# Graph network on one Trainium2 core: a head of three tiles in place of four in the second half of the adjacency stage

## What is computed

```python
h = relu(layernorm(x));  x = x + gcn2(relu(gcn1(h)))      # two GCN layers, the same edges
h = relu(layernorm(x))
w = silu(edge_attr @ We1 + be1) @ We2 + be2
m = w * (h[src] @ Wlin)
x = x + h + silu(segment_sum(m, dst) @ Wn1 + bn1) @ Wn2 + bn2
```

## The kernel before, in words

| blocks | windows | 2 tiles | 3 tiles | 4 tiles | 5 or more |
|---|---|---|---|---|---|
| 0 to 24 | 200 | 0 | 3 | 67 | 130 |
| 25 to 48 | 192 | 1 | 130 | 60 | 1 (the last window: 6) |

## Time and profile before

### The profile page before, as it was taken

One profiled execution on the slowest core, in us unless ns is written; L12 is line 12 of the kernel. 1 busy time (PEld: TensorE's weight loads), 2 busy tenths in 40 slices (PEclk: granted clock), 3 DMA queues, 4 the chain that ended last, 5 costly groups with the idle time before them and its releaser, 6 DMA issues.

```text
span 3517.3 us, 70075 instructions
## 1 busy us (share of the span) xinstructions
PE 2970.2 (84%) x19882; PEld 2165.5 (62%) x19883; DVE 2086.3 (59%) x4759; ACT 959.0 (27%) x2055; POOL 1494.5 (42%) x1601
## 2 busy tenths in 40 slices
PE   6979999999999969978877777778778778777777
PEld 4742456777777769955555555555555555555555
DVE  7999999999999844444443344433444334443333
ACT  5110234455666511122222222122122222122221
POOL 0000000000000000057777777777777777777774
PEclk8989999999999989978788888887788888888888
DMA  2000011222222269833333333333333333333332
GB/s 62 0 0 1 38 56 74 93 93 107 111 111 110 108 267 346 323 79 80 76 80 79 79 77 79 80 79 78 78 80 79 79 79 79 77 79 80 77 76 67
DMA packets 278864, 324.81 MB, mean 92 GB/s; under 512 B 231024, under 2 KB 238345, under 8 KB 266143
## 3 DMA queue, kind: packets, MB, share of 16 engines
q1 hardware_dynamic: 227518, 217.13, 18.6%
q0 software_dynamic: 51168, 106.07, 11.8%
HBM read 238.00 MB, written 85.09 MB: 92 GB/s over the span
## 4 chain that ended last, share of the span: by engine, by line
POOL 41%; PE 35%; issue 17%; DVE 5%; DVEq 1%; POOLq 1%; ACT 0%; DMA 0%; SPq 0%; ACTq 0%
POOL shared L497 41%; PE pb L1294 9%; PE pa L1294 9%; PE pc L1288 6%; PE pd L1288 5%; PE pd L1252 3%; PE pf L1254 1%; PE pb L1379 1%; DVE shared L952 1%; DVE loop L952 1%; PE pb L1506 0%; PE pa L1372 0%; DVEq L952 0%; PE pb L1262 0%; DVE loop L957 0%
## 5 line engine op out<-in xcount | busy, mean ns | idle before, releaser
L497 POOL DMA_INDIRECT shared<-lin_table,idx x1568 | 1479.6, 944 | 479.0 <-issue 477.5
L1115 DVE TENSOR_TENSOR shared<-pb,shared 128x512 f32<-128x512 f32 x392 | 252.4, 686 | 1171.8 <-DMA shared<-lin_table,idx 1171.8
L526 POOL DMA_DIRECT2D lin_table<-c x12 | 9.2, 770 | 1498.9 <-issue 1308.6
L1453 PE MATMUL pb<-we_sb,shared 128*128 128x128 f32 x3136 | 619.8, 359 | 0.0
L1453 PEld LDWEIGHTS pb<-we_sb,shared 128*128 128x128 f32 x3136 | 526.3, 254 | 119.6 <-issue 119.1
L729 ACT ACTIVATE shared<-pa,be_col 128x512 f32<-128x512 f32 x392 | 247.9, 683 | 1101.7 <-PE pa L1442 1101.7
L1449 PE MATMUL pb<-be_parts,ones 3*128 3x512 bf16 x392 | 177.9, 454 | 404.9 <-DVE shared L1115 404.5
L952 DVE TENSOR_SCALAR shared<-col_h,shared 128x784 bf16<-128x784 f16 x1092 | 402.7, 416 | 5.0 <-issue 4.5
L1449 PEld LDWEIGHTS pb<-be_parts,ones 3*128 3x128 bf16 x392 | 36.5, 93 | 467.8 <-issue 451.0
L1442 PE MATMUL pa<-shared,we_sb 64*128 64x512 f32 x784 | 306.8, 870 | 0.7 <-ACT shared L724 0.7
L1294 PE MATMUL pb<-shared,c 128*128 128x392 bf16 x1568 | 304.0, 329 | 1.6 <-DVE shared L952 0.9
(11 more groups left out here) (233 smaller groups left out, 3813.5 us busy)
## 6 DMA issues: line engine op xcount, KB each, us to landing
adjacency<-shared SPq DMA_DIRECT2D x49, 1568.0 KB, 5.6
shared<-adjacency SPq DMA_DIRECT2D x49, 1568.0 KB, 8.4
shared<-in_edge_attr_dram SPq DMA_DIRECT2D x195, 256.0 KB, 3.0
shared<-lin_table,idx POOLq DMA_INDIRECT x1568
lin_table<-c POOLq DMA_DIRECT2D x12, 256.0 KB, 6.9
out_dram<-xr SPq DMA_DIRECT2D x12, 256.0 KB
shared<-in_dst_dram SPq DMA_DIRECT2D x1, 512.0 KB
shared<-in_src_dram SPq DMA_DIRECT2D x1, 512.0 KB
```

The lines of the kernel that those rows point to most:

```text
L497: pool.indirect_dma_start(out=dest(s, j), out_offset=None, in_=table, in_offset=bass.IndirectOffsetOnAxis(ap=idx[:, s, j:j + 1], axis=0)). ...
L1115: dve.tensor_tensor(msgs[s % 2][:, h, :, :], pb[:, h, :].rearrange("p (i f) -> p i f", f=F), rows[:, h, :, :], ALU.mult).then_inc(msg_read ...
L1453: last = pe.matmul(pb[:, h, i * F:(i + 1) * F], act_t[:, h, i * P:(i + 1) * P], we2_sb[:, :], start=False, stop=(i == 3))
```

## The change

From block 25 on (SHORT) the head has three tiles (SHORT_HEAD). `head_columns(1)` and PE's second head part do one tile there. What a window has more than three is done as one tile by itself (`single`), and what is more than four in the loop of four. `sources` of the head is as wide as before (four tiles). The block loop is written twice, with 12 turns each: blocks 1 to 24 with the old form, blocks 25 to 48 with the new. The tables are written with two instructions each, one for each range of blocks.

```diff
+SHORT = 25
+SHORT_HEAD = 3
...
+        def late_heads(b, short):
+
+            return b * WB + SHORT * WB if short else b * (WB * T)
...
             for n in range(2):
                 dve.wait_ge(test_used, (n + 1) * UCOLS)
                 of = span_ps[n].rearrange("a (b w) -> a b w", w=WB)
-                to = windows[:, 0:NB, n, :]
-                if n == 0:
-                    dve.tensor_scalar(to, of, float(UNITS - HEAD), None, ALU.min).then_inc(windows_ready, 1)
-                else:
-                    dve.tensor_scalar(to, of, -float(HEAD), 0.0, ALU.add, ALU.max).then_inc(windows_ready, 1)
+                for blocks, head in ((slice(0, SHORT), HEAD), (slice(SHORT, NB), SHORT_HEAD)):
+                    to = windows[:, blocks, n, :]
+                    if n == 0:
+                        dve.tensor_scalar(to, of[:, blocks, :], float(UNITS - head), None, ALU.min).then_inc(windows_ready, 1)
+                    else:
+                        dve.tensor_scalar(to, of[:, blocks, :], -float(head), 0.0, ALU.add, ALU.max).then_inc(windows_ready, 1)
...
-            def build_block(b, i, k, first=False):
+            def build_block(b, i, k, first=False, short=False):
+                head = SHORT_HEAD if short else HEAD
...
                     def head_columns(j):
-                        for t in range(T):
+                        for t in range(head - T if j else T):
                             columns(head_col[w % 2][j][:, t, :], i, first_tile, j * T + t, w).then_inc(head_hot[j], 1)
...
                         for o in range(2):
+                            if short:
+                                dve.wait_ge(tile_hot[o][0], units[o])
                             dve.wait_ge(tile_hot[o][T - 1], units[o])
...
+                    def single(e, u, ahead):
+                        dve.reg_add(units[e], units[e], 1)
+                        dve.wait_ge(tile_used[e][0], units[e])
+                        columns(loop_col[e][:, 0, :], i, u, ahead, w)
+                        dve.wait_ge(tile_used[e][1], units[e])
+                        sources(loop_lo[e], iota_t, u, ahead, T).then_inc(tile_hot[e][0], 1)
+                        dve.sem_inc(tile_hot[e][1], 1)
+
                     with dve.If_lt(spans[w], spans[WB + w]):
-                        odd_pair(dve, lead, start, spans[w], spans[WB + w])
-                        with dve.If_ne(lead, 0):
-                            loop_pair(w % 2, first_tile, HEAD)
+                        if short:
+                            single(w % 2, first_tile, head)
+                            dve.reg_add(start, spans[w], 1)
+                        else:
+                            odd_pair(dve, lead, start, spans[w], spans[WB + w])
+                            with dve.If_ne(lead, 0):
+                                loop_pair(w % 2, first_tile, head)
                         with dve.If_lt(start, spans[WB + w]):
...
-            with nc.Fori(0, NB // 2, engines=bass.OrderedEngineSet([dve.engine]), hint_back_edge=True) as it:
-                build_block(it * 2 + 1, 1, it)
-                build_block(it * 2 + 2, 0, it + 1)
+            for turns, short in (((0, SHORT // 2), False), ((SHORT // 2, NB // 2), True)):
+                with nc.Fori(*turns, engines=bass.OrderedEngineSet([dve.engine]), hint_back_edge=True) as it:
+                    build_block(it * 2 + 1, 1, it, short=short)
+                    build_block(it * 2 + 2, 0, it + 1, short=short)
...
+                    def single(e):
+                        pe.reg_add(units[e], units[e], 1)
+                        pe.wait_ge(tile_hot[e][0], units[e])
+                        tile_counts(ps, loop_lo[e][:, :, 0], loop_col[e][:, 0, :]).then_inc(tile_used[e][0], 1)
+                        pe.wait_ge(tile_hot[e][1], units[e])
+                        pe.sem_inc(tile_used[e][1], 1)
+
                     with pe.If_lt(ranges[w], ranges[WB + w]):
-                        odd_pair(pe, lead, start, ranges[w], ranges[WB + w])
-                        with pe.If_ne(lead, 0):
-                            loop_pair(w % 2)
+                        if short:
+                            single(w % 2)
+                            pe.reg_add(start, ranges[w], 1)
+                        else:
+                            odd_pair(pe, lead, start, ranges[w], ranges[WB + w])
+                            with pe.If_ne(lead, 0):
+                                loop_pair(w % 2)
```

More of the change, by code:

```diff
@@ L54 @@
 assert N_NODES <= PAD_DST
+assert SHORT % 2 == 1 and SHORT_HEAD == T + 1
 def gnn_kernel(nc, x, src, dst, edge_attr, W1, b1, W2, b2, We1, be1, We2, be2, Wlin, Wn1, bn1, Wn2, bn2, out):
@@ L941, in _ @@
             lead, start = dve.alloc_register("lead_dve"), dve.alloc_register("start_dve")
-            dve.wait_ge(windows_ready, 2)
+            dve.wait_ge(windows_ready, 4)
             for t in range(HEAD):
@@ L975, in build_block @@
                     if w == 0 and not first:
-                        dve.wait_ge(head_hot[1], b * (WB * T))
+                        dve.wait_ge(head_hot[1], late_heads(b, short))
                         dve.sem_inc(passed, 1)
                         for o in range(2):
+                            if short:
+                                dve.wait_ge(tile_hot[o][0], units[o])
                             dve.wait_ge(tile_hot[o][T - 1], units[o])
@@ L1236, in _ @@
             pe.wait_ge(w_loaded, 16 * (N_W - 3))
-            pe.wait_ge(windows_ready, 2)
+            pe.wait_ge(windows_ready, 4)
             pe.sem_inc(hist_used, RING - 1)
@@ L1295, in tile_counts, with head_counts, build_block @@
                 return last
-            def head_counts(ps, n, w, j):
-                for t in range(T):
-                    pe.wait_ge(head_hot[j], n * T + (t + 1))
+            def head_counts(ps, b, w, j, short):
+                tiles = SHORT_HEAD - T if short and j else T
+                for t in range(tiles):
+                    if j:
+                        pe.wait_ge(head_hot[j], late_heads(b, short) + (w * tiles + t + 1))
+                    else:
+                        pe.wait_ge(head_hot[j], b * (WB * T) + (w * T + t + 1))
                     last = tile_counts(ps, head_lo[w % 2][:, :, j * T + t], head_col[w % 2][j][:, t, :],
-                                       first=(j == 0 and t == 0), end=(j == 1 and t == T - 1))
+                                       first=(j == 0 and t == 0), end=(j == 1 and t == tiles - 1))
                 return last.then_inc(head_used[j], 1)
-            def build_block(b, i, first=False):
+            def build_block(b, i, first=False, short=False):
                 window_spans(pe, ranges, b)
@@ L1309, in build_block @@
                     pe.sem_inc(passed, 1)
-                    head_counts(ps, b * WB + w, w, 0)
+                    head_counts(ps, b, w, 0, short)
                     def loop_pair(e):
@@ L1324, in build_block @@
                                 loop_pair(w % 2)
-                    head_counts(ps, b * WB + w, w, 1)
+                    head_counts(ps, b, w, 1, short)
                     if w > 0 and not first:
@@ L1333, in _ @@
             pe.wait_ge(split_ready[0], 2)
-            with nc.Fori(0, NB // 2, engines=bass.OrderedEngineSet([pe.engine]), hint_back_edge=True) as it:
-                build_block(it * 2 + 1, 1)
-                build_block(it * 2 + 2, 0)
+            for turns, short in (((0, SHORT // 2), False), ((SHORT // 2, NB // 2), True)):
+                with nc.Fori(*turns, engines=bass.OrderedEngineSet([pe.engine]), hint_back_edge=True) as it:
+                    build_block(it * 2 + 1, 1, short=short)
+                    build_block(it * 2 + 2, 0, short=short)
             pe.wait_ge(win_out, NW + 2)
```

11 lines of the change are left out of this document (6 added, 5 removed).

## The result

The changed kernel takes **3494.3 us** (median of 4 runs, 3492.9 to 3496.1) against 3518.1 for the kernel before beside it (3516.6 to 3520.3): ratio 0.9936, 95% interval 0.9924 to 0.9948. It is faster, by 23.8 us; the forecast was 31, and its range of 3475 to 3500 holds the time. The profiled execution took 3496.07, its span 3494.4.

The account below looks back on a forecast made before the run. PE's gapless matmuls were taken to bound blocks 25 to 48. The 42.9 us saved, less 10.8 for block steps, 0.5 for DVE, 0.5 for the second loop and 0.2 for tables, gave 31 us: 3487.6 us, range 3475 to 3500.

Parts of the forecast that it names:

- Tiles left out: Blocks 25 to 48: 641 tiles in place of 770, so PE loses 42.9 us on the path that sets the end.
- The step from block to block: PE's sequencer between blocks no longer covered by queued matmuls: loss of 10.8 us, bounds 0 and 14.4.
- The second loop: Step from the first block loop into the second: 0.5 us lost, bounds 0 and 2.2, a gain excluded.
- The branch and the single tile: Windows of four entering the branch body on both engines: 0 inside a block, upper bound 13 us.
- DVE's excess: Blocks where DVE's work exceeds PE's: 0.5 us in the sum, bounds 0 and 2.6.
- rival 2: DVE and PE, near equal, hold each other up: 25 us lost, 3501 us, or 3494 if half the blocks; chance 0.20.
- The tables: Two instructions of 0.55 us become four of about half the length: 0.2 us lost, bounds 0 to 0.5.
- The stages behind: Stages after the adjacency stage start earlier and keep their length; a change of length would prove the forecast wrong.
- Rival 1: All of the tiles' gain arrives, block steps being hidden: 3475.8 us, up to 3481 with small terms; chance 0.20.
- Rival 3: Each of 60 windows' jumps into fresh code stalls: at 1.5 us a window 47 us slower, 3566 us; chance 0.05.

Follow-up runs that it names:

- fourth_counts_pad: Changed kernel with lighter fourth tile, PE's load of 8 numbers instead of 16, and 64 never-run instructions between DVE's two loops: 3481.9 us, ratio 0.9888.
- ahead3: Changed kernel with PE's load of the next block's 16 bounds moved from the block's start to behind window 3: 3496.8 us, ratio 0.9940.
- two_loops: Kernel before with DVE's and PE's block loop each written twice, old form of block in both, no tile left out: ratio 1.0047.
- fourth: Changed kernel with the fourth tile's sources taken from the head's own tile and its columns put into the head's free buffer: ratio 0.9983.
- fourth_counts: Changed kernel with the lighter fourth tile and PE's load of 8 numbers instead of 16, no padding: 3500.8 us, ratio 0.9952.
- fourth_pad: Changed kernel with the lighter fourth tile and 64 never-run instructions between DVE's two loops: 3486.3 us, ratio 0.9912.

## Why the prediction was right, and where it was off

- **Tiles left out, 42.9 us: right to the tile.** 2035 `columns`, and fourth_counts_pad comes to within 10 us of the stretch that PE's work alone would take. The path was right too: PE's stream sets the stretch, and what was lost are waits in it.
- **The step from block to block: right in kind, mis-sized.** "I take 0.45 x 24 = 10.8 us; bounds 0 and 0.6 x 24 = 14.4". The gaps are 16.7 us, of which 1.8 are block 25's entry and 14.9 the other 23 steps. The place and the cause are the predicted ones: halving the load took 10 us from these gaps. At the even blocks the measured 0.47 is what was taken. The odd ones have 0.83, and there PE's sequencer has 0.55 us more to do, the turn of its loop. The rows that the sum was read from stand at the start of block 26, an even one, and so leave it out; the 0.60 of the earlier trace rows, put down to the branch, stands at block 15, behind such a turn. ahead3 adds that PE has so little handed over in windows of three tiles that the load bares it at another place as well.
- **The second loop: the term that failed most.** "The step from one loop into the other has no row [...] Taken: 0.5, nearer the bottom as the next code simply follows", with a top of 2.2. It cost 3.3 us of DVE's time at once, block 25 had 4.0 us of excess, eight times what was taken and above the top, and two_loops puts it on the second copy alone (3.8). "A gain there is excluded" held. The turns of the second loop had no term at all; in the changed kernel they stayed at 0.48 to 0.87 us, six of eleven as in the first loop (0.47 to 0.54), while in three other layouts (two_loops, fourth, fourth_counts) they took 2.0 to 2.6 and the odd blocks' excess was 12.8 to 27.2 us.
- **The branch and the single tile: taken as 0 inside a block, with a top of 13.** The even blocks lost 4.7 us of excess once the tile was made lighter (4.2 in fourth_pad), so it isn't hidden. fourth_pad is 8.4 us shorter than the changed kernel in all, but in the odd blocks and in block 25 the place of the code differs too. Which part of the tile costs it isn't shown: the 0.2 us of sources, the two waits and the unit count were taken out together. The bound was priced from the wrong side: before, 191 of the 192 compares at L1317 took 0.22 us, as windows with nothing for the body jump over it. In the changed kernel the 61 windows that enter the body pass this compare in 0.08 to 0.09 us and jump at the second one instead, 0.22 in most.
- **DVE's excess, 0.5:** rival 2 had blocks 25 to 31 held up by DVE. Those seven have 11.1 us of excess, 4.0 of it block 25's entry, the rest 0.7 to 1.8 us each; from block 40 on the even blocks are at 0.2 to 0.3. Its sign, PE waiting for L965 or L960, is in the trace at block 25 (1.7 us) and once more (0.2); the other waits that the view names are put down to ACT (10.0) and to issue (0.8). How much of the excess is DVE's tile work no run separates.
- **The tables, 0.2:** right. Two instructions of 0.55 us became four of 0.34 to 0.35.
- **The stages behind.** "I am wrong if the stages behind change their length, since nothing here touches them." They did: 3.5 us shorter behind the last block, by layout.
- In sum the excess was 24.3 where 11.8 was forecast (10.8, 0.5 and 0.5), and 3.5 + 1.0 us of it came back elsewhere for reasons that have nothing to do with tiles. The forecast missed by 6.7 us. That it missed by no more, and that the range up to 3500 held, is in part luck: without the 3.5 us the time is 3497.8, and with the turns of fourth, whose odd blocks had 15 us more of excess, it would have lain above 3500.
- **The rivals.** Rival 1 (no step costs anything) fell by the gaps. Rival 3 (the branch stalls at each of 60 windows) has no trace: the even blocks 26 to 46 hold 28 of these windows and have 7.6 us of excess in all. But the place of the code, which made it plausible, was at work at the loop's entry and turn instead of at the windows' branches. By the rule of the Trainium skill that I named beside it ("Runtime: NRT & Kernel Launch", section Instruction fetch mechanics) a taken branch out of the fetched window stops for a fetch. The stops of 2.0 to 2.6 us at the turns fit that, while no view here shows a fetch or where the fetched window ends; that fetching is the cause is argued, not shown.
- The Trainium skill ("TensorE: Matmul & The Clock Gate", section Architectural detail) gives TensorE a queue of 64 instructions. Read by itself, that would have made the block step free; the trace has a gap at each of the 24 steps, 16.7 us in all. In this kernel the sequencer was only one or two windows ahead, held by its wait in each window, and then by the load of 1.10 us.

What stays open: which place of the code makes a turn cost 0.5 or 2.5 us, and whether the changed kernel's own turn is a lucky one; how the 24.3 us divide between PE's load, PE's turn, DVE's entry and the single tile, since no run took each away alone; and the last 10 us of excess, of which block 25's entry has 2.5 and block 48 1.6.

## What to carry to other kernels

When work is taken from the engine that fills a stage, reckon what its sequencer does between two pieces of work against what is left to cover it: here 43 us of matmuls were removed, 24 us of waits stood in their place, and 4 of these belong to the new loop itself. A loop written twice isn't free: look at the engine's time between the branch and the first instruction of the next turn, and try the same code at another place before believing a result of a few tenths of a per cent, for better or worse. And split the stretch into blocks with and without the suspected event: in the run fourth the even and odd blocks told apart what the total time had hidden.

## What the runs showed of the hardware

- **A load of registers that meets a store ends with it.** 16 numbers took 1.10 us, 8 took 0.59 and one 0.32; while the 1.57 MB store was under way 16 took up to 2.57 us (in 67 of 67 loads over 1.2 us the load ended with the store, to within 0.6 us) and 8 up to 1.02. In the kernel before the same load cost 1.07 us a block behind window 2 and nothing behind window 3 or at the block's start.
- **The place of code sets what a loop's turn costs**, 0.5 to 1.2 or 2.4 to 2.6 us on DVE for the same loop, and 64 instructions that never run moved it. PE's sequencer stood only 0.06 to 0.12 us between branch and next instruction in the second loops too; its whole turn took 0.55 us.
- **Falling out of one loop into the next cost DVE's sequencer 3.3 to 3.6 us (2.9 to 3.1 with the 64 instructions between) and PE's 0.15 us**, the one time that it happens. The turn at the same place took 0.49 on DVE before.
- **A compare took PE's sequencer 0.22 us where it jumped and 0.08 where it didn't** (L1317 and L1352, blocks 25 to 48).
